# Four graph layers: the scores of attention layers 2 and 3 made inside the layer before, and both layers in one block

## Chip, cores, metric

One NeuronCore of one Trainium2 chip runs the whole program. The metric is device time in microseconds of one execution; smaller is better.

## The reference

Four layers over N = 8192 nodes with F = 128 features, each followed by `x = layernorm(x + layer(x))`. Layer 0 takes the maximum over neighbours. Layer 1 is graph attention with a threshold on the weights. Layers 2 and 3 are graph attention:

```python
Wh = h @ W
e = leaky_relu((Wh @ a_1)[:, None] + (Wh @ a_2)[None, :], 0.2)
attention = softmax(where(adj > 0, e, NEG), axis=1)
h_prime = attention @ Wh
return elu(h_prime)
```

Each row's score is a dot product of that row with `W @ a`, for `a_1` and for `a_2`; the column scores enter through factors that need their greatest value over all nodes.

## The kernel before

The node features live in `X`, 128 partitions by T = 64 tiles of 128 features. Rows of a 0/1 mask, transposed and in one byte, were written to DRAM (`mask_t`) by layer 0.

Engines here are PE (TensorE), DVE (VectorE), ACT (ScalarE), POOL (GpSimd) and SP, which issues most transfers. Each engine's order is written out by hand, and semaphores join them. Every layer is a `Phase`, which ends with barriers of all engines.

**Layer 1** (`threshold_layer`) has a preparing stage and then S = 8 strips of 1024 target rows. A strip walks 64 steps j. At each, DVE makes `w` (line 1481: the weights of tile j for 1024 targets) into a ring of six, and PE multiplies (line 1223). Beside it run the denominators of the next strip (ACT makes `above`, DVE masks it, PE adds it up) and the thresholds (ACT makes `u`, DVE masks it, line 1356). Between two strips POOL makes the next strip's limit in five small instructions (lines 1119 to 1129). PE turns the limits, ACT copies them to `ell`, makes `u`, and DVE masks `u` before the last two `w` of the old strip. The results of strip c are added to `X` during strip c + 1, where their mean and variance go to `stats` (DVE steps j = 38 to 42). Normalising them waits for the next layer.

**Layers 2 and 3** (`attention_layer`, called twice) each begin with a preparing stage, then have 16 chunks of 512 targets. The preparing stage loads W and a, and turns all of `X` on PE into `XT` (ACT copies it, 16 pieces). PE makes the scores of each tile from it (line 1572), with dummy matmuls between. In layer 2 it also normalises the 64 tiles (line 1630). DVE sums `XT` for the mean row (line 1654). It then takes the greatest score (line 1660), POOL joins the partitions, and ACT makes the factors `E` and `G`. In a chunk, DVE makes `w` (line 1888) into a ring of WR = 8, and PE multiplies by `GX` (line 1773). At j = 24, 28 and 38 DVE finishes the chunk before: `post`, `post_rest`, `standardise` (line 1868). In chunk 0 DVE also makes `GX` (`weigh`, line 1873). POOL makes `lone_part`, one instruction per chunk (line 1738). ACT is used little there.

Of the kernel before, what the change touches and what calls it, by code (L numbers as in the profile page):

```python
# [5 lines left out]
F32 = mybir.dt.float32  # L6
# [860 lines left out]
def threshold_layer(nc, W1, a_src, a_dst, mask_t, xt_rows, X, stats, rstd, ident, sel):  # L867

    with ExitStack() as ctx:
# [22 lines left out]
        post_bank = ctx.enter_context(nc.psum_tensor("post_bank", [P, H, CI], F32))  # L892
        den_in = [sem(f"den_in{b}") for b in range(2)]
# [8 lines left out]
        with ExitStack() as pctx:  # L902
            psb = lambda n, s: pctx.enter_context(nc.sbuf_tensor(f"{n}_1", s, F32))
            XT, WT, A3, U3, sdh = psb("XT", [P, N]), psb("WT", [P, F]), psb("A3", [P, 3]), psb("U3", [P, 3]), psb("sdh", [P, T, 3])
            B, rest, dm, nb, v = psb("B", [P, T]), psb("rest", [P, T]), psb("dm", [P, 1]), psb("nb", [P, 3]), psb("v", [P, T])
            banks = [ps[:, h, :] for ps in (acc, den_ps, row_ps, post_bank) for h in range(H)]
            w_in, step, eps_made, rstd_made = sem("w_in"), sem("prep_step"), sem("eps_made"), sem("rstd_made")
# [7 lines left out]
            def _(sp):  # L915
                sp.dma_start(Wn[:, :], W1).then_inc(w_in, 16)
                sp.dma_start(A3[:, 0:1], a_src).then_inc(w_in, 16)
                sp.dma_start(A3[:, 1:2], a_dst).then_inc(w_in, 16)
                for n in range(2):
                    load(sp, den_m, den_in, n)  # L920
# [13 lines left out]
            def _(pe):  # L934

                def weights():
# [4 lines left out]
                    pe.wait_ge(u_sb, 1)  # L941

# [31 lines left out]
                last.then_inc(sd_ps, 1)  # L974

            @block.scalar
            def _(act):
                nc.scalar.preload_act_table_set(LN_EXP)
                act.wait_ge(eps_made, 1)
                nc.scalar.activation(rstd[:, :], stats[:, :, 1], ACT.Ln, bias=epsc[:, 0:1]).then_inc(rstd_made, 1)  # L980
                act.wait_ge(rstd_made, 1)
                nc.scalar.activation(rstd[:, :], rstd[:, :], ACT.Exp, scale=-0.5).then_inc(rstd_made, 1)
                for g in range(NG):
                    act.wait_ge(tr, g + 1)
                    nc.scalar.activation(XT[:, g * CI:(g + 1) * CI], banks[g % 4][:, :], ACT.Copy).then_inc(ev, 1)
                act.wait_ge(nb_sb, 1)
# [3 lines left out]
                nc.scalar.activation(qcol[:, :], zcol[:, :], ACT.Exp, scale=-0.8).then_inc(egb, 1)  # L990

            @block.vector
            def _(dve):
# [10 lines left out]
                dve.wait_ge(rstd_made, 2)  # L1004
# [5 lines left out]
                for g in range(1, T // NORM):  # L1010
                    normalise(g)
                s.did(nc.vector.memset(tiny[:, :], TINY))
# [37 lines left out]
        xt = sb("xt", [P, W], F32)  # L1050
        above = sb("above", [P, AS, H, GT, CI], FP8)
# [60 lines left out]
        def _(pool):  # L1112
            for c in range(S):
# [901 lines left out]
```

## Time and profile before

| | us |
|---|---|
| median of 3 runs (4797.67 to 4809.75) | 4803.89 |
| the profiled execution | 4804.22 |
| its span | 4802.5 |
| PE busy (91% of the span) | 4376.7 |
| DVE busy (89%) | 4257.5 |
| ACT busy (47%) | 2267.8 |
| POOL busy (24%, nearly all in layer 0) | 1163.7 |

The span runs from the first to the last instruction. By the timeline, layer 0 ends at about 1617 us, layer 1's first products start at 1730 us, and its last at 2875 us. Layer 2's products run from 2941 to 3836 us and layer 3's from 3894 to 4789 us. An engine's busy share is a mean over stages that differ, so the stages are read one by one.

### The profile page before, as it was taken

The numbers are of one execution on the slowest core, as the hardware profiler recorded it, in microseconds if no ns is written. First come the engines' busy times: TensorE is split into PE (matmuls) and PEld (weight loads), VectorE is DVE, ScalarE is ACT, GpSimd is POOL, SyncE is SP. The second block draws the span as 40 slices with busy tenths as digits, with TensorE's granted clock in tenths as the row PEclk, the third lists the DMA queues.
The fourth block names the chain that finished last, engine by engine and source line by source line (L and its number), as shares of the span: only waits on it lengthen the run. The fifth ranks groups of instructions, "written<-read, shape, count | busy, mean of one in ns | idle before, by whom it ended". The sixth has DMA issues, their size and how long they took to land. (4 is left out here: it accounts for less than half of the span.)

```text
span 4802.5 us, 67836 instructions
## 1 busy us (share of the span) xinstructions
PE 4376.7 (91%) x22391; PEld 2133.7 (44%) x22391; DVE 4257.5 (89%) x7884; ACT 2267.8 (47%) x2494; POOL 1163.7 (24%) x1195
## 2 busy tenths in 40 slices
PE   5888888888888579999999998999999989999998
PEld 3444554444444324333443344444444454444444
DVE  7999999999999778888888888999999869999998
ACT  4677777677766398899888841000000010000000
POOL 6677677667677100000000000000000000000000
PEclk7999999999999789999999998999999989999999
DMA  8788888778876232333333212222222022222220
GB/s 318 264 275 270 267 275 273 257 260 276 266 265 211 98 132 106 118 119 127 111 117 115 109 57 113 82 76 75 82 83 81 3 111 79 79 83 104 83 84 7
DMA packets 181702, 709.78 MB, mean 148 GB/s; under 512 B 31168, under 2 KB 39872, under 8 KB 132224
## 3 DMA queue, kind: packets, MB, share of 16 engines
q1 hardware_dynamic: 110816, 566.01, 34.3%
q0 software_dynamic: 33760, 73.21, 4.7%
q10 hardware_dynamic: 36864, 67.13, 3.7%
q8 instruction: 158, 2.59, 0.2%
q14 instruction: 104, 0.85, 0.1%
HBM read 630.59 MB, written 79.82 MB: 148 GB/s over the span
## 5 line engine op out<-in xcount | busy, mean ns | idle before, releaser
L1773 PE MATMUL bank<-w,GX 128*128 128x512 f32 x4096 | 1768.1, 593 | 4.8 <-DVE w L1888 4.8
L1888 DVE SCALAR_TENSOR_TENSOR w<-q,E,m 128x512 f32<-128x512 f32 x2048 | 1471.8, 759 | 130.1 <-PE bank L1773 40.2
L1773 PEld LDWEIGHTS bank<-w,GX 128*128 128x128 f32 x4096 | 777.5, 190 | 975.2 <-issue 975.1
L367 POOL DMA_INDIRECT ring<-x_ext,idx x1051 | 1053.3, 1002 | 481.6 <-issue 329.7
L1223 PE MATMUL acc<-w,GX 128*128 128x512 f32 x2048 | 938.1, 604 | 67.5 <-DVE w L1481 64.3
L521 PE MATMUL sums<-lone,xs 128*128 128x512 fp8e4 x3000 | 744.9, 385 | 142.2 <-DVE top L625 127.9
L431 ACT ACTIVATE stage<-tp 128x1024 fp8e4<-128x1024 uint16 x512 | 523.1, 1023 | 424.6 <-PE tp L484 408.7
L625 DVE TENSOR_TENSOR top<-top,sums 128x512 f32<-128x512 f32 x968 | 618.4, 678 | 38.9 <-PE sums L521 38.3
L1481 DVE SCALAR_TENSOR_TENSOR w<-q,E,u 128x1024 f32<-128x1024 f32 x512 | 635.1, 1275 | 1.9 <-PE acc L1223 1.8
L1223 PEld LDWEIGHTS acc<-w,GX 128*128 128x128 f32 x2048 | 371.4, 190 | 566.0 <-issue 411.8
L416 ACT ACTIVATE lone<-first_ps 128x1024 fp8e4<-128x1024 f32 x512 | 521.2, 1018 | 38.3 <-PE first_ps L507 37.5
L521 PEld LDWEIGHTS sums<-lone,xs 128*128 128x128 bf16 x3000 | 276.9, 98 | 566.6 <-issue 278.6
L1254 ACT ACTIVATE above<-q,nd 128x1024 fp8e4<-128x1024 f32 x488 | 516.4, 1140 | 0.0
L1265 ACT ACTIVATE u<-ell,ndd 128x1024 fp8e4<-128x1024 f32 x448 | 478.0, 1140 | 43.6 <-DVE w L1481 43.2
L1785 ACT ACTIVATE num<-bank 128x512 f32<-128x512 f32 x32 | 19.1, 597 | 1005.4 <-PE bank L1773 1005.4
L1738 POOL TENSOR_TENSOR lone_part<-mean_w,nohas 128x512 f32<-128x512 f32 x32 | 37.5, 1174 | 1583.7 <-DVEq L1846 1560.8
L484 PE MATMUL tp<-ident_b,adjb 128*128 128x128 bf16 x4096 | 328.2, 226 | 76.1 <-DVE X L649 43.0
L507 PE MATMUL first_ps<-stage,firsts 128*128 128x512 fp8e4 x1022 | 312.0, 388 | 2.2 <-ACT lone L416 2.2
L484 PEld LDWEIGHTS tp<-ident_b,adjb 128*128 128x128 bf16 x4096 | 255.4, 101 | 109.3 <-DVE X L649 46.3
L630 DVE TENSOR_TENSOR ring<-ring 128x384 f32<-128x384 f32 (+2 forms) x512 | 260.8, 509 | 22.2 <-DMA ring<-x_ext,idx 17.7
L1789 ACT ACTIVATE ex<-ex 128x512 f32<-128x512 f32 x32 | 20.2, 630 | 540.6 <-DVE ex L1847 540.6
L1119 POOL TENSOR_TENSOR den<-den,qcol 128x8 f32<-128x8 f32 x8 | 9.5, 1193 | 1045.9 <-ACT den L1300 1045.9
(252 smaller groups left out, 3199.9 us busy)
## 6 DMA issues: line engine op xcount, KB each, us to landing
adjb<-in_adj SPq DMA_DIRECT2D x256, 1024.0 KB
m<-mask_t SPq DMA_DIRECT2D x128, 1024.0 KB, 4.9
mask_t<-stage ACTq DMA_DIRECT2D x256, 256.0 KB
den_m<-mask_t SPq DMA_DIRECT2D x64, 1024.0 KB, 7.0
keep_m<-mask_t SPq DMA_DIRECT2D x64, 1024.0 KB, 4.9
ring<-x_ext,idx POOLq DMA_INDIRECT x1051
z<-row_scores SPq DMA_DIRECT2D x30, 256.0 KB, 4.7
xt_rows<-XT SPq DMA_DIRECT2D x8, 512.0 KB, 4.0
```

What stands on the lines that cost most here:

```text
L367: pool.indirect_dma_start(ring[:, s, :], None, x_ext, bass.IndirectOffsetOnAxis(ap=idx[:, k, s:s + 1], axis=0)).then_inc(done, 16)
L416: nc.scalar.activation(lone[:, b, :, :], first_ps[:, :, :], ACT.Relu, saturate=False).then_inc(lone_made, 1)
L431: nc.scalar.activation(stage[:, q, e * TRB:(e + 1) * TRB, k * P:(k + 1) * P], tp[e % 2][:, :, :].bitcast(U16), ACT.Sign, saturate=False).t ...
L484: last = nc.tensor.transpose(tp[e % 2][:, i, :], low_half[:, j // PW, j % PW:j % PW + P], ident_b[:, :])
L521: last = nc.tensor.matmul(out[:, a, :], xs[:, part_, 2 * n + a, :], lone[:, b, a, :], start=(part_ == 0), stop=(part_ == 2))
L625: nc.vector.tensor_tensor(out=top[:, a, :], in0=top[:, a, :], in1=sums[:, a, :], op=ALU.max).then_inc(sums_used[a], 1)
L1223: last = nc.tensor.matmul(acc[:, h, :], GX[:, j, :], w[:, n % WR1, h, :], start=(j == 0), stop=(j == T - 1))
L1254: nc.scalar.activation(above[:, n % AS, :, i, :], qb[:, c % 2, :, :], ACT.Sign, bias=nd[:, j:j + 1], scale=-1.0, saturate=False).then_inc( ...
L1265: nc.scalar.activation(u[:, n % US, :, i, :], ell[:, c % 2, :, :], ACT.Sign, bias=ndd[:, j:j + 1], saturate=False).then_inc(keeps_made, 1)
L1481: nc.vector.scalar_tensor_tensor(out=w[:, n % WR1, :, :], in0=qb[:, c % 2, :, :], scalar=E[:, j:j + 1], in1=u[:, n // GT % US, :, j % GT, ...
L1773: last = nc.tensor.matmul(acc[b][:, :], GX[:, j, :], w[:, j % WR, :], start=(j == 0), stop=(j == T - 1))
L1888: nc.vector.scalar_tensor_tensor(out=w[:, j % WR, :], in0=q, scalar=E[:, j:j + 1], in1=m[:, b, j, :], op0=ALU.max, op1=ALU.mult).then_inc( ...
```

## The change

The preparing stages of layers 2 and 3 are gone, and both layers stand in one `Phase` and one block (`attention_layers`; l = 0 and 1). What they made is made elsewhere:

- **In layer 1's preparing stage**: W and a of layer 2 are loaded, and `U_next`, the product of W and a spread over all partitions, is made.
- **In layer 1's strips**: ACT makes `rstd` of strip c - 1 at j = 50 (`spread`). POOL runs `prepare_next` for a strip whose rows are final: it normalises eight tiles, adds them to a running sum and makes both scores by a product and halvings, 26 instructions. It follows the five limit instructions of strip c, for strip c - 2. One more call stands behind the loop. The eighth strip is left to the next phase, where DVE normalises it and makes the scores that the greatest value needs.
- **In layer 2's chunks**: POOL makes the two products of layer 3's scores and the running sum, three instructions a chunk, and ACT adds up the products in eight activations a chunk.
- **In chunk 0 of both layers**: PE turns the scores, makes the mean row, and in layer 2 also layer 3's weights. The masks of layer 3's first two chunks are loaded during layer 2's last two.

```diff
+def threshold_layer(nc, W1, a_src, a_dst, mask_t, xt_rows, X, stats, rstd, ident, sel, lastrow, following):
...
+            def prepare_next(c):
+
+                col = slice(c * KC, (c + 1) * KC)
+                pool.wait_ge(rstd_made, 2 * (c + 1))
+                pool.wait_ge(stats_made, KC * (c + 1))
+                for t in range(c * KC, (c + 1) * KC):
+                    nc.gpsimd.tensor_scalar(X[:, t, :], X[:, t, :], stats[:, t, 0:1], rstd[:, t:t + 1], ALU.subtract, ALU.mult).then_inc(rows_normed, 1)
+                pool.wait_ge(rows_normed, KC * (c + 1))
+                for i in range(2):
+                    half = slice(c * KC + i * TC, c * KC + (i + 1) * TC)
+                    pool.wait_ge(x_summed, 2 * c + i + 1)
+                    nc.gpsimd.tensor_tensor(out=x_sum[:, :, :], in0=x_sum[:, :, :], in1=X[:, half, :], op=ALU.add).then_inc(x_summed, 1)
+                for k in range(2):
+                    own.do(nc.gpsimd.tensor_tensor(out=prod[:, :, :], in0=X[:, col, :], in1=U_next[:, k, :].unsqueeze(1).to_broadcast([P, KC, F]), op=ALU.mult))
+                    h = F // 2
+                    while h > 1:
+                        own.do(nc.gpsimd.tensor_tensor(out=prod[:, :, 0:h], in0=prod[:, :, 0:h], in1=prod[:, :, h:2 * h], op=ALU.add))
+                        h //= 2
+                    own.do(nc.gpsimd.tensor_tensor(out=scores_next[:, k, col], in0=prod[:, :, 0], in1=prod[:, :, 1], op=ALU.add))
...
                 nc.gpsimd.tensor_tensor(out=limit[:, :], in0=over[:, :], in1=logs[:, :], op=ALU.add).then_inc(limit_made, 1)
+                if c >= 2:
+                    prepare_next(c - 2)
+            prepare_next(S - 2)
...
+                    if c > 0 and j == 50:
+                        spread(c - 1)
...
         @block.gpsimd
         def _(pool):
...
+            greatest(0)
+            pool.wait_ge(rows_normed, KC)
+            for k in range(2):
+                score(k, NC - 2 + k, 0, 0)
+            for k in range(2):
+                add_rows(0, NC - 2 + k, k + 1)
...
+            for c in range(NC - 1):
+                if c + 2 < NC:
+                    pool.wait_ge(post_used, c + 2)
+                    for_lone(0, c + 2, c % 2)
+                pool.wait_ge(x_normed, (c + 1) * TC)
+                pool.wait_ge(scored, OPENED + c * 2 * TC)
+                for k in range(2):
+                    score(k, c, 1, k)
+                add_rows(1, c, c + 3)
+            greatest(1)
...
         @block.tensor
         def _(pe):
...
+                    if first and j == 16:
+                        turn_scores(l)
+                        mean_of_rows(l)
+                    if first and j == 24:
+                        mean_of_products(l)
+                    if first and l == 0 and j == 36:
+                        turn_next_weights()
+                    if first and l == 0 and j == 44:
+                        score_rows()
...
         @block.vector
         def _(dve):
...
+            def greatest_score(l):
...
+                s.do(nc.vector.tensor_tensor(out=last_prod[:, 0:tiles, :], in0=X[:, at, :], in1=Us[l][:, 1, :].unsqueeze(1).to_broadcast([P, tiles, F]), op=ALU.mult))
+                s.do(nc.vector.tensor_reduce(scores[l][:, 1, at], last_prod[:, 0:tiles, :], axis=AXX, op=ALU.add))
+                if l:
+                    dve.wait_ge(scored, SCORED)
+                nc.vector.tensor_reduce(dms[l][:, :], scores[l][:, 1, :], axis=AXX, op=ALU.max).then_inc(next_dm, 1)
```

On POOL, in layer 1, these rows follow the limit of strip c in the changed kernel (`prod` and `scores` are the products and the scores of the next layer):

```order
L1179 TENSOR_TENSOR limit<-over,logs 128x8
L1148 TENSOR_SCALAR X<-X,stats,rstd 128x128 x8
L1153 TENSOR_TENSOR x_sum<-x_sum,X 128x512 x2
L1155 TENSOR_TENSOR prod<-X,U 128x1024
L1158 TENSOR_TENSOR prod<-prod 128x8x64
L1158 TENSOR_TENSOR prod<-prod 128x8x32
L1158 TENSOR_TENSOR prod<-prod 128x8x16
```

Before, the limit was the last row, and the first of the next strip's five came next.

On DVE, between layers 1 and 2, the kernel before has these rows between the statistics of the last strip and the first `w`:

```order
L1630 TENSOR_SCALAR X<-X,stats,rstd 128x128 x56
L1654 TENSOR_REDUCE zc<-XT 128x1
L1655 TENSOR_SCALAR zrep<-zc 128x128
L1658 COPY sdh<-bank_2 128x192
L1660 TENSOR_REDUCE dm<-sdh 128x1
L1663 TENSOR_SCALAR nb<-D 128x1 x2
```

The changed kernel has these in that place, and the same but for the first between layers 2 and 3:

```order
L2031 TENSOR_SCALAR X<-X,stats,rstd 128x128 x8
L1985 TENSOR_TENSOR last_prod<-X,U 128x1024
L1986 TENSOR_REDUCE scores<-last_prod 128x8
L1989 TENSOR_REDUCE dm_2<-scores 128x1
L1992 TENSOR_SCALAR nb_2<-D_2 128x1 x2
L1973 TENSOR_TENSOR GX<-X,G_2 128x8x127
```

The normalising of 56 tiles and the long sum left DVE, and the product and sum of the last tiles came.

## Rows read from the trace of the kernel before

**Rows 1.** Page, costliest groups: busy us, mean ns, idle before with its releaser.
```profile
L1773 PE MATMUL bank<-w,GX 128*128 128x512 f32 x4096 | 1768.1, 593 | 4.8 <-DVE w L1888 4.8
```

**Rows 2.** Windows: length, busy us of each engine (instructions), PEclk, DMA share, GB/s.
```profile
2160.00:2308.00 148.00, 139.32 (x578) 58.49 (x577) 125.94 (x134) 133.68 (x131) 4.90 (x5) 1.00 0.32 117
...
2999.00:3054.00 55.00, 55.00 (x136) 24.84 (x135) 50.62 (x86) 2.77 (x6) 1.14 (x1) 1.00 0.24 81
...
3836.00:3894.00 58.00, 40.23 (x307) 35.24 (x306) 19.12 (x41) 16.54 (x29) 0.38 (x1) 0.77 0.38 152
...
2940.00:2943.00 3.00, 2.07 (x3) 1.07 (x4) 2.97 (x5) 1.24 (x2) 0.00 (x0) 0.50 0.38 86
```

**Rows 3.** Timeline, layer 1 to layer 2: start us, length us, engine, line, operation [idle before].
```profile
2889.18 0.64 DVE L1442 BATCH_NORM_AGGREGATE stats<-bn 128x2 f32<-128x6 f32 x8
...
2893.39 2.14 DVE L1630 TENSOR_SCALAR X<-X,stats,rstd 128x128 f32<-128x128 f32 x8 [1.37 <-ACT rstd L1613]
...
2932.11 0.24 DVE L1660 TENSOR_REDUCE dm<-sdh 128x1 f32<-128x64 f32 x1
...
2933.21 0.38 ACT L1618 ACTIVATE E<-sdh,nb 128x64 f32<-128x64 f32 x1 [10.72 <-DVEq L1665]
...
2938.65 0.69 ACT L1802 ACTIVATE z<-bank,D 128x512 f32<-128x512 f32 x1 [1.03 <-PE bank L1753]
...
2940.03 1.42 DVE L1888 SCALAR_TENSOR_TENSOR w<-q,E,m 128x512 f32<-128x512 f32 x2 [1.99 <-ACT q L1807]
...
2940.93 2.04 PE L1773 MATMUL bank<-w,GX 128*128 128x512 f32 x2 [2.38 <-DVE w L1888]
```

**Rows 4.** Timeline, layer 2 to layer 3.
```profile
3844.37 1.12 DVE L1868 TENSOR_SCALAR X<-X,mv,rs 128x128 f32<-128x128 f32 x4 [0.60 <-ACT rs L1795]
...
3894.22 1.19 PE L1773 MATMUL bank<-w,GX 128*128 128x512 f32 x1 [2.38 <-DVE w L1888]
```

**Rows 5.** Groups by line, VectorE.
```profile
L1434 DVE SCALAR_TENSOR_TENSOR X<-hp,X 128x1024 f32<-128x1024 f32 x8 | 9.7, 1215 | 0.0
...
L656 DVE TENSOR_REDUCE codes<-X 128x4 f32<-128x512 f32 x16 | 10.8, 677 | 0.0
```

**Rows 6.** Timeline, POOL: before layer 1, in its first strip and in a later strip.
```profile
1562.57 19.73 POOL L404 TENSOR_TENSOR X<-X,adjb 128x512 f32<-128x512 f32 x15 [1.83 <-DMA ring<-x_ext,idx]
...
1718.61 0.21 POOL L1121 TENSOR_TENSOR den<-den,den 128x8 f32<-128x8 f32 x1
...
2299.41 1.12 POOL L1121 TENSOR_TENSOR den<-den,den 128x8 f32<-128x8 f32 x1
```

**Rows 7.** Timeline, four w instructions with a POOL instruction beside them, and without.
```profile
3072.69 1.15 POOL L1738 TENSOR_TENSOR lone_part<-mean_w,nohas 128x512 f32<-128x512 f32 x1 [54.67 <-DVEq L1846]
...
3072.86 3.52 DVE L1888 SCALAR_TENSOR_TENSOR w<-q,E,m 128x512 f32<-128x512 f32 x4
...
3798.60 2.73 DVE L1888 SCALAR_TENSOR_TENSOR w<-q,E,m 128x512 f32<-128x512 f32 x4
```

**Rows 8.** Timeline, the end of a strip of layer 1.
```profile
2303.04 1.06 POOL L1129 TENSOR_TENSOR limit<-over,logs 128x8 f32<-128x8 f32 x1
...
2311.47 1.23 DVE L1356 SCALAR_TENSOR_TENSOR u<-u,keep_m 128x1024 int32<-128x1024 int32 x1 [7.43 <-ACT u L1265]
...
2313.95 3.70 PE L1223 MATMUL acc<-w,GX 128*128 128x512 f32 x8 [1.00 <-DVE w L1481]
...
2328.16 1.23 DVE L1356 SCALAR_TENSOR_TENSOR above<-above,den_m 128x1024 int32<-128x1024 int32 x1 [5.29 <-DMA den_m<-mask_t]
```

**Rows 9.** Timeline, ScalarE late in the last strip of layer 1.
```profile
2842.78 4.27 ACT L1265 ACTIVATE u<-ell,ndd 128x1024 fp8e4<-128x1024 f32 x4 [2.69 <-DVE w L1481]
```

**Rows 10.** Timeline, one chunk of layer 2.
```profile
3005.46 1.05 PE L1761 MATMUL bank<-Wa,num 128*128 128x129 f32 x8
...
3030.74 17.77 DVE L1888 SCALAR_TENSOR_TENSOR w<-q,E,m 128x512 f32<-128x512 f32 x25
...
3048.75 13.49 DVE L1888 SCALAR_TENSOR_TENSOR w<-q,E,m 128x512 f32<-128x512 f32 x16 [0.24 <-PE bank L1773]
```

More of the change, by code:

```diff
@@ L1721, in _ @@
                     hold(sp, q_ready, it * 2 + b + 1)
[L1722 to L1732 removed]
+                    load_rows(0, it * 2 + b + 2, b)
@@ new lines, in _ @@
+                    masks(it * 2 + b, it * 2 + b + 2, b)
+            for b in range(2):
+                masks(NC - 2 + b, b, b)
+            turned(1)
+            sp.wait_ge(q_ready, NC)
+            load_rows(1, 1, 1)
+            with sp.Fori(0, NC // 2 - 1) as it:
+                for b in range(2):
+                    hold(sp, q_ready, it * 2 + (NC + b + 1))
+                    load_rows(1, it * 2 + b + 2, b)
+                    masks(it * 2 + (NC + b), it * 2 + b + 2, b)
+                    store(it * 2 + b)
@@ L1776, in _ @@
             w_in_order = Tally(pe, w_made)
-            chunks(pe, chunk, post)
+            for l in range(2):
+                if l:
+                    pe.wait_ge(num_ready, NC - 1)
+                    pe.wait_ge(eps_made, 3)
+                chunk(l, 0, 0, True)
+                with pe.Fori(0, NC // 2 - 1) as it:
+                    chunk(l, it * 2 + 1, 1, False)
+                    chunk(l, it * 2 + 2, 0, False)
+                chunk(l, NC - 1, 1, False)
+                post(l, NC - 1)
@@ L1807, in chunk, with sum_scores @@
                 nc.scalar.activation(qb[:, b, :], z[:, b, :], ACT.Exp, scale=-0.8).then_inc(q_ready, 1)
-                if not first:
-                    take(c - 1, 1 - b)
-                    expo(c - 1)
-                    spread(c - 1)
-            def end(c, b):
-                take(c, b)
-                expo(c)
-                spread(c)
-            nc.scalar.preload_act_table_set(LN_EXP)
-            written_out(chunk, end)
+            def sum_scores(l, parts, before):
+                for n, (k, c, kind) in enumerate(parts):
+                    act.wait_ge(prod_made, before + n + 1)
+                    for i in range(TC):
+                        t = c * TC + i
+                        nc.scalar.activation(prod[:, k, i, :], prod[:, k, i, :], ACT.Copy, accum_out=scores[l][:, kind, t:t + 1]).then_inc(scored, 1)
@@ L1907, in program @@
+            for t in range(T - KC, T):
+                nc.vector.tensor_scalar(X[:, t, :], X[:, t, :], stats[:, t, 0:1], rstd[:, t:t + 1], ALU.subtract, ALU.mult).then_inc(rows_normed, 1)
+            for l in range(2):
+                greatest_score(l)
+                for c in range(NC):
+                    chunk(l, c, c % 2)
+                post(l, NC - 1)
+                post_rest(l, NC - 1)
+                standardise(l, NC - 1)
 def program(nc, x, adj, W1, a1, W2, a2, W3, a3, out):
```

540 lines of the change are left out of this document (286 added, 254 removed).

## Prediction

> **What bounds the kernel now.** I read the page first, then the busy time by windows to find the stages, then the timeline at their borders.
>
> In layers 2 and 3 the page gives 1768.1 us to the products of 2048 steps, 0.863 us a step, and PE waited 4.8 us for them in all [rows 1]. A window inside a chunk shows PE busy for 55.00 of 55 us and DVE for 50.62 [rows 2]. So PE sets these chunks, and DVE has 4.4 us to spare in each.
>
> Between the layers PE does nothing of this. The last instruction of layer 1's tail on DVE ends at 2889.8 us and the first product of layer 2 starts at 2940.93 [rows 3]. Layer 2's tail ends at 3845.5 and layer 3 starts at 3894.22 [rows 4]. These two stretches, 51 and 49 us, are what the change attacks.
>
> In layer 1 a strip takes about 148 us, in which PE is busy for 139.32, ACT for 133.68 and DVE for 125.94 [rows 2]. No engine has much room. At the end of a strip DVE waits 7.43 us for `u`, masks it, makes the last two `w`, and PE, its ring run dry, waits 1.00 us for them [rows 8]. This place matters, because `prepare_next` starts there.
>
> **Layer 1 to layer 2.** The phase starts as before, and DVE's first eight tiles are normalised by 2893.39 + 2.14 = 2895.5 [rows 3]. Then come, one behind the other: the product of eight tiles, 1.22 (the form 128x1024 with two inputs), its sum, 2 x 0.68 = 1.36 [rows 5]; from the start of the greatest value to ACT's first factor 1.10; two factors, 0.7 together; from `z` to the first `w` 1.38; to the first product 0.90 [rows 3]. That is 6.7 us, so 2902.2. POOL has two products of rows queued behind `greatest(0)`, just when DVE wants its first `weigh`. I add 1.5 for that, about one POOL instruction. Layer 2 starts at 2903.7, and 2940.93 - 2903.7 = 37.2 us go.
>
> **Layer 2 to layer 3.** No phase ends here. From 3845.5: product of four tiles 0.6, sum 0.68, then the same 1.10 + 0.7 + 1.38 + 0.90, and 1.5 for POOL, together 6.9, so 3852.4. 3894.22 - 3852.4 = 41.8 us go. Both savings: 79.0 us. The row scores and the mean row aren't on this path: they are made inside chunk 0, and needed by chunk 1 some 50 us later. ACT and SP wait in line for them there, but the rows of chunk 1 need only a turn at j = 16 and two transfers.
>
> **What chunk 0 gains in work.** PE gets 18 short passes in layer 2 (one turn of scores, eight for the mean row, two for its product, seven for the next weights) and 11 in layer 3. Eight such passes take 1.05 us [rows 10], so 2.3 + 1.4 = 3.7 us. DVE loses POOL's extra instructions in the same chunk, but PE's extra work and its slow start cover them: its clock is granted at 0.50 just after the idle stretch before [rows 2], and I take that to be so in both kernels.
>
> **What POOL costs DVE.** This is the disputed term. A POOL instruction of 512 columns takes 19.73 / 15 = 1.32 us and one of eight columns 0.21 us with DVE elsewhere, but the same eight columns take 1.12 us beside DVE's masks and `w` [rows 6]. The two engines hold each other up. Four `w` take 2.73 us alone and 3.52 us with one POOL instruction of 512 columns beside them, so DVE loses 0.79 us [rows 7]. The eight-column instructions cost it nothing that I can see.
>
> The Trainium skill ("SBUF — State Buffer", section "SBUF: two separate sides") calls the port pair that DVE and POOL share an exclusive lock, held for the whole instruction. By it DVE would lose up to POOL's whole time with the port, more than my 0.79; the last rival is what that would do here.
>
> `prepare_next` on POOL, from rows 6 by a straight line (0.2 us and 0.0022 us a column): eight of 128 columns 0.45 each, two of 512 at 1.3, and for each of two scores 2.4 + 1.3 + 0.7 + 0.45 + five short ones 1.3. That is 3.6 + 2.6 + 12.3, with their waits some 20 us. It runs six times behind a limit. The limit ends at 2304.1 [rows 8]; the first ten instructions fit the stretch in which DVE is idle, but the 1024-column product runs from about 2311 to 2313, over the mask at 2311.47 (1.5 us late), and the 512-column halving meets the `w` behind it (0.8), the next halvings the second one (0.5). PE is waiting for exactly these, and ACT waits for PE. So I take 3 us a strip, 18 us in all. Later in the strip DVE waits 5.29 us for a mask [rows 8] and for ACT elsewhere, so I let the rest be absorbed. The bounds: nothing (DVE's idle takes it all), and 0.79 us per 512 columns for all of it with none absorbed; the 26 instructions hold some 6100 columns (8 x 128, 2 x 512 and 2 x 2032), so 9.4 us a strip and 57 us for six.
>
> The seventh call stands at the end of layer 1. It can start when ACT has made `u` of the last group but one, at 2847.1 [rows 9]. Slowed to one short instruction per DVE instruction it would end near 2877, ahead of 2889.8 [rows 3], so it costs nothing. If it didn't, each us beyond would be a us of the kernel. `spread` puts two short activations in a place where ACT waits for `w`, and costs nothing. Layer 1's preparing stage gets three small loads and a turn: 0.5 us.
>
> **Layer 2's chunks.** Three POOL instructions follow `standardise`, 3 x 0.79 = 2.4 us. After that place DVE makes 25 `w` in 17.77 us, 0.711 each, where PE takes 0.863, and then waits for PE [rows 1, 10]. So it had been 25 x 0.15 = 3.8 us behind a full ring of 8 x 0.863 = 6.9, with 3.1 us left. 2.4 fits in 3.1, and in DVE's 4.4 us a chunk. I take 0.5 us in all for the first chunks. ACT's eight activations a chunk find ACT idle (busy for 2.77 us of 55).
>
> **The sum.** 4804.2 - 79.0 + 3.7 + 18 + 0.5 + 0.5 = 4747.9. The profiled execution is within 0.4 us of the median, so nothing is corrected: 4748 us, 1.2% faster.
>
> **The rivals.**
>
> 1. POOL in layer 1 is free. DVE is idle for 148 - 125.94 = 22 us of a strip, and a ring of six `w` stands between it and PE. Against it, PE already waits at the very place. 4748 - 18 = 4730.
> 2. POOL costs its full price in layer 1, 9.4 us a strip and none absorbed: 4748 - 18 + 57 = 4787. For it: all three engines are over 85% busy. Against it: DVE is idle for some 6 of the first 7 us in which `prepare_next` runs, and waits again later.
> 3. The ring of eight runs dry in layer 2. If a product of real rows costs DVE the whole 1.3 us, three cost 3.9 against 3.1: 0.8 us in 14 chunks, 4748 + 11 = 4759. It lies in the forecast's own range.
> 4. Slower: the port is held for all of POOL's 20 us, and the strip grows by it, since the late masks delay the loads that SP issues behind them and so the next masks. Six strips give 120: 4748 - 18 + 120 = 4850. It decides from (79.0 - 4.7) / 6 = 12.4 us a strip upward. Against it: 0.79 of 1.15 us is what one such instruction cost, and part of the work meets an idle DVE.
>
> **How the numbers follow.** The forecast, with its own range of 4735 to 4772 (about 1 to 7 us a strip, the third rival in it), gets 0.68. POOL free gets 0.12, the full price 0.11, and the fourth rival or any other way to end near the old time or above 0.09. A range from 4722 to 4788 leaves out the last, half of the full price, and a little below: a faster restart of PE would put the free case under 4730. A change of 0.3%, 14 us, is about what a measurement of this kernel can tell from none. Faster (below 4790) holds the forecast, the free case and most of the full price: 0.87. Within 0.3% I give 0.06, slower 0.07.
>
> **What would show it.** The start of layer 2's products should lie 13 to 14 us behind the last tail instruction of layer 1, and layer 3's 7 us behind layer 2's. The strips of layer 1 should show 148 us grown to about 151 from the second on, with a longer PE wait for `w` just behind each limit. PE should be busy throughout the chunks of layer 2, and their length stay 55.6 us. I am wrong if a strip grows by over 6 us, if POOL's last `prepare_next` ends after DVE's last statistics, or if layer 2's chunks are longer than layer 3's.

## The result and the profile after

The changed kernel takes 4757.6 us (median of 4 runs, 4745.5 to 4762.7) where the kernel before takes 4804.4: the ratio is 0.990, with a 95% interval of 0.9877 to 0.9922. That is 47 us less. Run again beside other experiments it took 4756.2 (0.9904, 0.9888 to 0.9921). The forecast was 4748, its range 4722 to 4788. Two executions among the experiments, one of e1's kernel (7800 us) and one of e4's (8445 us), fell in a slow state and are left out of every median.

The profiled execution of the changed kernel is its fastest run, 4745.5 us with a span of 4742.9. Of its costliest groups these lines of the page answer to [rows 1]; columns are busy us, mean ns, and idle time before with its releaser.

```profile
L1802 PE MATMUL bank<-w,GX 128*128 128x512 f32 x4096 | 1769.7, 593 | 27.4 <-DVE w L2015 27.4
L2015 DVE SCALAR_TENSOR_TENSOR w<-q,E,m 128x512 f32<-128x512 f32 x2048 | 1478.5, 773 | 101.1 <-PE bank L1802 35.7
...
L1276 PE MATMUL acc<-w,GX 128*128 128x512 f32 x2048 | 947.6, 609 | 77.3 <-DVE w L1544 74.4
...
L1687 POOL TENSOR_TENSOR prod<-X,U_next 128x512 f32<-128x512 f32 x31 | 227.3, 7352 | 230.6 <-DVE X L1968 223.6
```

The products of layers 2 and 3 (L1802) cost what they did. The two stretches between layers shrank. The timeline from layer 1 to layer 2, for [rows 3]:

```profile
2902.90 0.64 DVE L1505 BATCH_NORM_AGGREGATE stats<-bn 128x2 f32<-128x6 f32 x8
...
2905.01 0.53 POOL L1700 MEMSET x_sum<- 128x512 f32 x1 [5.02 <-POOLq L113]
...
2911.57 0.22 DVE L1989 TENSOR_REDUCE dm<-scores 128x1 f32<-128x64 f32 x1
...
2916.56 0.38 POOL L1698 PARTITION_ALL_REDUCE D<-dm  x1 [11.03 <-issue]
...
2920.11 13.47 PE L1802 MATMUL bank<-w,GX 128*128 128x512 f32 x26 [13.84 <-DVE w L2015]
...
2928.43 3.36 POOL L1687 TENSOR_TENSOR prod<-X,U 128x512 f32<-128x512 f32 x2 [11.49 <-issue]
```

The tail ends at 2903.54 and the first product starts 16.6 us later, where it was 51.1. One thing stands out: the maximum `dm` is ready at 2911.79, but POOL's all-reduce starts at 2916.56, and POOL stood for 11.03 us before it with "issue" as the reason. From layer 2 to layer 3, for [rows 4]:

```profile
3826.63 1.11 DVE L1968 TENSOR_SCALAR X<-X,mv,rs 128x128 f32<-128x128 f32 x4 [0.60 <-ACT rs L1834]
...
3829.58 0.38 POOL L1698 PARTITION_ALL_REDUCE D<-dm  x1 [21.95 <-DVE dm L1989]
...
3833.12 2.90 PE L1802 MATMUL bank<-w,GX 128*128 128x512 f32 x3 [12.42 <-DVE w L2015]
```

5.4 us from tail to product, where it was 48.7. What was paid for this shows in layer 1. The groups of lines from the second strip's limit to the tail's end, before (L1223) and after (L1276), with the same columns as the page:

```profile
L1223 PE MATMUL acc<-w,GX 128*128 128x512 f32 x1832 | 836.3, 602 | 55.2 <-DVE w L1481 52.2 <-ACT num L1236 2.6
```

```profile
L1276 PE MATMUL acc<-w,GX 128*128 128x512 f32 x1832 | 845.2, 608 | 65.5 <-DVE w L1544 62.8 <-ACT num L1289 2.6
```

This stretch grew from 1034.2 to 1054.4 us, by 20.2. PE waits 10.3 us more for `w`, and its same 1832 products take 8.9 us longer. The second number is not a wait: the products themselves ran slower. The border of a strip, in the timeline, for [rows 8]:

```profile
2303.10 6.24 POOL L1148 TENSOR_SCALAR X<-X,stats,rstd 128x128 f32<-128x128 f32 x8
2309.42 3.48 POOL L1153 TENSOR_TENSOR x_sum<-x_sum,X 128x512 f32<-128x512 f32 x2
2312.86 3.33 POOL L1155 TENSOR_TENSOR prod<-X,U 128x1024 f32<-128x1024 f32 x1
...
2310.49 1.29 DVE L1419 SCALAR_TENSOR_TENSOR u<-u,keep_m 128x1024 int32<-128x1024 int32 x1 [7.44 <-ACT u L1318]
2311.70 7.77 DVE L1544 SCALAR_TENSOR_TENSOR w<-q,E,u 128x1024 f32<-128x1024 f32 x3
...
2314.04 1.98 PE L1276 MATMUL acc<-w,GX 128*128 128x512 f32 x4 [2.08 <-DVE w L1544]
2317.32 1.98 PE L1276 MATMUL acc<-w,GX 128*128 128x512 f32 x4 [1.30 <-DVE w L1544]
...
2333.77 3.63 PE L1276 MATMUL acc<-w,GX 128*128 128x512 f32 x4 [2.05 <-DVE w L1544]
```

Three `w` take 7.77 us beside POOL's additions and products, against some 3.7 without. Four products of PE take 1.98 us at 2317, but 3.63 at 2333.77. The windows around that place (length, busy us of PE, PEld, DVE, ACT and POOL, PEclk, DMA share, GB/s) say why:

```profile
2324.00:2333.70 9.70, 7.33 (x29) 4.14 (x28) 5.59 (x6) 9.70 (x11) 9.23 (x7) 1.00 0.85 324
2333.70:2337.10 3.40, 3.33 (x4) 1.17 (x4) 3.40 (x4) 3.40 (x5) 3.17 (x4) 0.50 0.00 0
2337.10:2345.00 7.90, 7.90 (x46) 3.10 (x46) 7.90 (x11) 7.90 (x8) 0.33 (x1) 1.00 0.14 31
```

Right behind the third wait the granted clock stands at 0.50, which is 1.2 in place of 2.4 GHz, for 3.4 us, and PE loses half of them, 1.7 us. In slices of 2 us the changed kernel shows six such stretches in layer 1, the kernel before none until layer 1's tail. Six times 1.7 is 10.2 us, and PE's busy time in the stretch from the second limit to the tail's end rose by 9.9 us, from 968.9 to 978.8, of which 8.9 are on the products.

So the change of the profiled execution, part by part: layer 1 +20.2; its end -34.5; layer 2's chunks +3.1; layer 2's end -43.3; layer 3 +2.0. Together -52.5 us. The execution of before that was profiled came 6.5 us later into layer 1's second strip, with nothing of the change in that part; over all the profiles of this study that moment lies between 1846.5 and 1862.9 us. It is left out of every comparison of parts below; the medians contain it.

### The profile page after: what moved, and what is told of

Same layout as the page of the kernel before. It is cut to its first block and busy times, and to the rows that moved or that the text cites. A ratio compares the mean times of both kernels' runs of the same rounds, so it can differ in the third digit from the quotient of the medians.

```text
span 4742.9 us, 66895 instructions
## 1 busy us (share of the span) xinstructions
PE 4303.7 (91%) x21712; PEld 2072.7 (44%) x21839; DVE 4294.5 (91%) x7813; ACT 2293.9 (48%) x2747; POOL 1668.6 (35%) x1430
## 5 line engine op out<-in xcount | busy, mean ns | idle before, releaser
L1802 PE MATMUL bank<-w,GX 128*128 128x512 f32 x4096 | 1769.7, 593 | 27.4 <-DVE w L2015 27.4
L1802 PEld LDWEIGHTS bank<-w,GX 128*128 128x128 f32 x4096 | 776.7, 190 | 993.8 <-issue 989.6
L1276 PE MATMUL acc<-w,GX 128*128 128x512 f32 x2048 | 947.6, 609 | 77.3 <-DVE w L1544 74.4
L1544 DVE SCALAR_TENSOR_TENSOR w<-q,E,u 128x1024 f32<-128x1024 f32 x512 | 665.2, 1336 | 0.1
L1276 PEld LDWEIGHTS acc<-w,GX 128*128 128x128 f32 x2048 | 373.6, 191 | 580.6 <-issue 409.2
L1169 POOL TENSOR_TENSOR den<-den,qcol 128x8 f32<-128x8 f32 x8 | 5.6, 704 | 883.5 <-ACT den L1361 883.5
L1687 POOL TENSOR_TENSOR prod<-X,U_next 128x512 f32<-128x512 f32 x31 | 227.3, 7352 | 230.6 <-DVE X L1968 223.6
L1828 ACT ACTIVATE ex<-ex 128x512 f32<-128x512 f32 x32 | 20.2, 631 | 563.8 <-DVE ex L1944 563.8
```

The costliest lines, as they stand in the source:

```text
L1276: last = nc.tensor.matmul(acc[:, h, :], GX[:, j, :], w[:, n % WR1, h, :], start=(j == 0), stop=(j == T - 1))
L1544: nc.vector.scalar_tensor_tensor(out=w[:, n % WR1, :, :], in0=qb[:, c % 2, :, :], scalar=E[:, j:j + 1], in1=u[:, n // GT % US, :, j % GT, ...
L1802: last = nc.tensor.matmul(acc[b][:, :], GX[:, j, :], w[:, j % WR, :], start=(j == 0), stop=(j == T - 1))
```

## The experiments

All start from the changed kernel. "Strips" are the distances between the first POOL instructions of one limit and the next (L1169), the second to the seventh. "Layer 1" runs from the second limit to the end of the tail on DVE; "products" and "waits" are the busy and the idle time of PE's `acc` group in it, as in the two lines above; "layer 2" runs from its first product to layer 3's. "Dips" are the stretches at half clock inside layer 1's strips, most of them 3.4 us long; one each in e11 and e5 and two in e3 are twice that.

```
kernel              strips (us)                          layer 1  products  waits  dips  layer 2  median
before              147.7 147.6 147.6 148.5 147.5 147.5   1034.2    836.3    55.2     0    953.3  4804.4
changed             147.6 150.5 150.4 151.8 150.9 150.6   1054.4    845.2    65.5     6    913.0  4757.6
e11 changed again   147.6 150.5 150.2 151.8 152.7 150.3   1055.7    844.5    67.1     5    920.6  4756.2
e2 no POOL work     147.7 147.7 147.7 149.0 147.7 147.8   1035.3    837.1    55.0     1    920.6  4743.5
e7 standardise only 147.6 147.6 147.9 149.1 147.6 148.4   1036.1    836.3    56.5     0    920.8  4734.8
e12 no products     147.7 148.8 150.8 151.8 148.8 150.4   1048.8    844.4    61.7     5    913.0  4752.5 (one run)
e3 products twice   147.7 154.7 155.2 155.8 155.1 154.4   1083.5    853.0    84.5    10    913.1  4789.5
e4 23 us later      147.7 153.9 153.8 155.1 153.8 153.8   1070.4    845.7    81.5     4    913.2  4766.4
e5 turned maximum   147.7 150.4 150.4 151.7 152.6 150.4   1056.3    843.9    68.2     4    920.7  4749.2
e6 products first   147.7 147.9 148.9 149.2 147.9 147.8   1046.7    838.4    64.2     1    920.7  4742.7
e8 e5 and e6        147.7 147.8 147.8 149.2 147.8 148.1   1045.7    838.9    64.0     1    920.6  4743.4
e9 all three        147.7 147.7 147.7 149.2 147.9 147.9   1045.3    838.9    63.8     1    913.9  4735.6
e10 e9, all-reduce  147.6 147.7 147.9 149.2 147.9 147.9   1045.3    839.1    63.4     1    913.4  4744.5
```

Ratios to the kernel before, with their intervals: e1 (e12's kernel, timed) 0.989, 0.9872 to 0.9907; e2 0.9861, 0.9836 to 0.9886; e3 0.9965, 0.9951 to 0.9978; e4 0.9922, 0.99 to 0.9943; e5 0.9878, 0.9861 to 0.9894; e6 0.9866, 0.9849 to 0.9882; e7 0.9843, 0.9826 to 0.986; e8 0.9866, 0.9846 to 0.9885; e9 0.9854, 0.9837 to 0.987; e10 0.9879, 0.9862 to 0.9895; the changed kernel as above.

### Is the loss in layer 1 POOL's, and of which work?

**e2, none of it.**

```diff
-                    nc.gpsimd.tensor_scalar(X[:, t, :], ... ).then_inc(rows_normed, 1)
+                pool.sem_inc(rows_normed, KC)
-                    nc.gpsimd.tensor_tensor(out=x_sum[:, :, :], ... ).then_inc(x_summed, 1)
+                    pool.sem_inc(x_summed, 1)
-                for k in range(2):
-                    own.do( ... products, halvings ... )
```

> The changed kernel with all seven calls of prepare_next emptied (no standardising, no running sum, no products; their semaphores are still raised, in their places), so layer 2 works on rows that are not standardised and on scores of zero. This leaves ACT's spread in layer 1 and the new borders as they are. Theory A and Rival C of the first kernel: strips of layer 1 back at 147.5 to 147.8, the last strip with the tail back at 147.8, in all 20 us less than the changed kernel, about 4737 us. Rival D, part of the 20 us in layer 1 isn't POOL's but comes of ACT's two added operations at step 50 or of DVE's separate semaphore steps: strips stay at 148.3 or more. POOL's all-reduce at the border of layers 1 and 2 should no longer start late, if what delayed it was the work before it: then another 4.8 us less; if it is a change of POOL's configuration of fixed length behind the border, it stays.

The strips are back at 147.7 to 149.0 and layer 1 is back at 1035.3: all but 1.1 of the 20.2 us are POOL's work. The all-reduce still started late, 10.89 us behind POOL's memset, so the delay isn't the work ahead of it. The median fell by 14 us and not by 20. In the two traces layer 2 took 7.6 us more; more on this below. How many of the timed executions had that isn't known.

**e1 and e12, without products and halvings.**

```diff
                     nc.gpsimd.tensor_tensor(out=x_sum[:, :, :], ... ).then_inc(x_summed, 1)
-                for k in range(2):
-                    own.do( ... products, halvings ... )
```

> The changed kernel with the products and their halvings left out of prepare_next (both score columns of all seven calls, so layer 2's scores are zeros from a memset; the standardising and the running sum stay). Each call of POOL falls from about 34 to about 10 us. In the changed kernel a strip of layer 1 takes 150.4 to 150.9 us where it took 147.5 to 147.7 before, and the last strip with the tail 4.9 us more. Theory A, that of the prediction (what counts is what meets DVE's mask and the refilling of the ring in the first 15 us of a strip, and the product and the halvings are what meets them): the strips fall to about 148.2, the total by some 14 to 17 us against the changed kernel. Rival B, the eight standardising operations, which come first, carry the delay: the strips stay at 149.5 or more, the total falls by less than 8 us. Rival C, every microsecond of POOL costs alike wherever it lies (3.0 us for 34, 0.09 each): strips at 148.5, total -14. A and C are told apart by the two other kernels of this call.

Timed, it took 4751.5 us, only 6 below the changed kernel. Neither theory A nor C had given that, and B, which had, falls with e7 below. Its strips are read from e12, the same kernel:

> The kernel without products and halvings once more, for a trace at full clock: each call of prepare_next keeps its eight standardising operations and the two 512-column adds of the running sum (products and scores left out, scores zero). Theory F (only POOL's two-input operations hold DVE up): the two adds take 3.5 of the 27 to 28 us of two-input work, so strips at 147.9 to 148.2 against 147.6 to 147.9 without them and 150.4 to 150.9 with all. Rival: the first two-input operations behind the border carry most of the loss, as they meet the mask: strips at 149 or more.

Theory F had given 147.9 to 148.2, and that isn't what came: the strips are of two kinds, 148.8 twice and 150.4 to 151.8 three times. The rival is near. The five strips with a call average 150.12 us, 2.15 above e2's 147.97, where the changed kernel's 150.83 are 2.86 above. So two of POOL's 18 two-input operations, the first two behind the border, carry three quarters of the loss in a strip. DVE was busy for 886.3 us in layer 1, only 7.4 more than without POOL's work (878.9 in e2), while layer 1 is 13.5 us longer.

The two kinds differ in the clock. The 148.8 have no dip, the others have one or two. At the border the first three `w` take 4.67 us in e12, and 3.67 before:

```profile
2624.93 4.67 DVE L1538 SCALAR_TENSOR_TENSOR w<-q,E,u 128x1024 f32<-128x1024 f32 x3
```

```profile
2312.62 3.67 DVE L1481 SCALAR_TENSOR_TENSOR w<-q,E,u 128x1024 f32<-128x1024 f32 x3
```

POOL's additions make one of them 1.0 us late. That is enough to make PE's wait at the border 2.04 to 2.29 us, where it is 1.00 without them. So a strip grows by 1.1 us where no dip follows, and by 2.6 to 3.1 where one or two do. Here are three of these six borders:

```profile
2176.13 5.40 PE L1270 MATMUL acc<-w,GX 128*128 128x512 f32 x8 [2.29 <-DVE w L1538]
...
2478.47 3.70 PE L1270 MATMUL acc<-w,GX 128*128 128x512 f32 x8 [2.05 <-DVE w L1538]
...
2627.27 5.40 PE L1270 MATMUL acc<-w,GX 128*128 128x512 f32 x8 [2.05 <-DVE w L1538]
```

Eight products in 5.40 us at the first and the third, and in 3.70 at the second: the dip's 1.7 us can be read off the row. A dip came at four of the six borders, and the length of the wait doesn't decide it, since one wait of 2.05 had none behind it and the next of 2.05 had one. What decides isn't settled.

**e7, the standardising alone.**

```diff
-                    nc.gpsimd.tensor_tensor(out=x_sum[:, :, :], ... ).then_inc(x_summed, 1)
+                    pool.sem_inc(x_summed, 1)
-                for k in range(2):
-                    own.do( ... products, halvings ... )
```

> The changed kernel with only the eight standardising operations left in each call of prepare_next: running sum, products and halvings are left out (scores and running sum zero from a memset). Theory F: these operations cost DVE nothing, strips of layer 1 at 147.6 to 147.9, as with all of POOL's work left out, total about 4743 us, some 14 below the changed kernel. Rival H: 6.2 of 34 us of the work remain, so strips at 148.2 and 4 us more in all than with none of it.

Strips at 147.6 to 149.1 and layer 1 at 1036.1 us: POOL's one-input operations cost next to nothing, whatever POOL's busy time. Rival H falls.

**e3, products and halvings twice.**

```diff
-                for k in range(2):
+                for k in (0, 1, 0, 1):
                     own.do(nc.gpsimd.tensor_tensor(out=prod[:, :, :], ...
```

> The changed kernel with the products and halvings of each prepare_next made twice (the same result is written a second time). Each call grows from about 34 to about 57 us; the added 23 us lie 35 to 58 us behind the start of a strip. Theory A (the loss is at the strip's border alone): strips grow by less than 0.5 us over the changed kernel's 150.4 to 150.9, the total by less than 4 us beside what the last call adds, which now ends after layer 1's tail (2899.99 in the changed kernel, tail to 2903.54) and holds up the border to layer 2 by some 20 us or more, since beside unbroken two-input operations of DVE it runs three times slower. Rival C (every microsecond of POOL costs alike): strips grow by 2.0 us, to 152.6. The prediction's fourth rival (DVE stands for as long as POOL has an operation in hand): strips grow by 23 us.

The added 23 us of POOL cost 3.8 to 4.9 us a strip, more than the first 34 did. Theory A falls in its strict form: the border isn't the only place where the loss is. The prediction's fourth rival falls too: DVE doesn't stand for all of POOL's time. The last call ended behind the tail and the first product came 27 us after it, as said.

**e4, the same work 23 us later.**

```diff
                 if c >= 2:
+                    pool.wait_ge(w_made, c * T + 10)
                     prepare_next(c - 2)
```

> The changed kernel with one wait added ahead of the first six calls of prepare_next: POOL begins when DVE has made the tenth tile of the strip, some 23 us behind the strip's first, when the ring of tiles is full again. The work is the same 34 us. Theory A: the strips fall from 150.4 to 150.9 to about 148.2 and the total by about 12 us. Rival C: the strips and the total stay. Rival E, the work costs more in the middle of a strip, where DVE's two-input operations follow each other without a gap and POOL gets the port late: POOL's call takes over 60 us, and strips grow.

The opposite of theory A: the strips grow to 153.8 to 155.1, and the call costs 6.2 us instead of 3. Its timeline shows POOL's instructions and DVE's beside them:

```profile
2501.22 16.53 POOL L1148 TENSOR_SCALAR X<-X,stats,rstd 128x128 f32<-128x128 f32 x8 [35.65 <-DVE w L1545]
2517.84 4.08 POOL L1153 TENSOR_TENSOR x_sum<-x_sum,X 128x512 f32<-128x512 f32 x2
2521.88 3.34 POOL L1155 TENSOR_TENSOR prod<-X,U 128x1024 f32<-128x1024 f32 x1
```

```profile
2504.59 3.73 DVE L1545 SCALAR_TENSOR_TENSOR w<-q,E,u 128x1024 f32<-128x1024 f32 x3
...
2518.49 2.29 DVE L1545 SCALAR_TENSOR_TENSOR w<-q,E,u 128x1024 f32<-128x1024 f32 x1
2520.71 2.28 DVE L1420 SCALAR_TENSOR_TENSOR u<-u,keep_m 128x1024 int32<-128x1024 int32 x1
2522.92 5.59 DVE L1545 SCALAR_TENSOR_TENSOR w<-q,E,u 128x1024 f32<-128x1024 f32 x2
```

Beside POOL's standardising three `w` take 3.73 us, as ever. Beside its additions and products each takes 2.3 to 2.8: the two engines go in turn, DVE's 1.2 us behind POOL's 1.1, which is the lock for a whole instruction that the prediction cited. The Trainium skill ("SBUF — State Buffer", section "Who interferes with whom") says that a DVE instruction with two SBUF inputs contends with a POOL instruction that reads SBUF. For POOL's two-input instructions these rows agree. The one-input ones read SBUF as well, and here they waited for DVE (16.53 us for eight that take 6.24 at the border) but did not hold it up.

**e6, products first.** If the border is the cheap place, because DVE stands there for 7.4 us, then the two-input work should lie there, and the standardising behind it:

```diff
-                if c >= 2:
-                    prepare_next(c - 2)
-            prepare_next(S - 2)
+                if c >= 3:
+                    multiply(c - 3)
+                if c >= 2:
+                    standardise(c - 2)
+            multiply(S - 3)
+            standardise(S - 2)
+            multiply(S - 2)
```

> The changed kernel with POOL's order turned round in layer 1: behind a strip's limit it now adds, multiplies and halves the rows that it standardised one strip earlier (call c - 3), and standardises the rows of call c - 2 behind that; the last strip does both. The work is the same, its place is moved by 6.3 us: in the changed kernel POOL standardises in the 7.4 us in which DVE stands at a strip's border and begins the two-input operations when DVE is back. The earlier kernels showed strips at 147.6 to 147.9 without POOL's work, 150.4 to 150.9 with it, 155 with the products twice, and 153.9 with the work begun 23 us late, where each of DVE's two-input operations beside one of POOL's took 2.3 us instead of 1.2 while beside POOL's standardising it stayed at 1.2. Theory F (a two-input operation of POOL holds up a two-input operation of DVE for its whole length, one-input operations don't): six us more of POOL's two-input time fall where DVE waits, so the strips fall to about 149.3, the total by 7 to 12 us. Rival H (only the busy time of POOL counts, whatever the operation): strips stay at 150.4 to 150.9.

```profile
2301.14 2.61 POOL L1155 TENSOR_TENSOR x_sum<-x_sum,X 128x512 f32<-128x512 f32 x2
2303.71 2.36 POOL L1157 TENSOR_TENSOR prod<-X,U 128x1024 f32<-128x1024 f32 x1
2306.15 6.22 POOL L1160 TENSOR_TENSOR prod<-prod 128x512 f32<-128x512 f32 x6
...
2308.56 1.29 DVE L1425 SCALAR_TENSOR_TENSOR u<-u,keep_m 128x1024 int32<-128x1024 int32 x1 [7.43 <-ACT u L1324]
```

The strips fall to 147.8 to 149.2, further than the 149.3 expected, and close to e2's. DVE is hardly less delayed (it is busy for 910.0 us in layer 1, against 914.6), but PE's waits in the first 40 us of a strip add up to 4.3 or 4.4 us in place of 6.1 in the first three (2.08, 1.30, 0.24, 0.40 and 2.05), where they were 3.0 before, and there is one dip in place of six. Products fall from 845.2 to 838.4 us. Of the 12.5 us of loss that are left, 9.4 lie in the last strip, in which the products of two calls now run in mid-strip: 157.2 us from its limit to the tail's end, against 147.8 before.

### The start of layer 2

**e5, the maximum without POOL.**

```diff
-            greatest(0)
             pool.wait_ge(rows_normed, KC)
+            pool.wait_ge(w_made, 8)
...
+                    pe.wait_ge(next_dm, 1)
+                    nc.tensor.transpose(banks[6][:, 0:P], dms[0][:, 0:1].to_broadcast([P, P]), ident[:, :]).then_inc(dm_turned, 1)
...
+                    dve.wait_ge(dm_turned, 1)
+                    nc.vector.tensor_reduce(Ds[0][:, 0:1], banks[6][:, 0:P], axis=AXX, op=ALU.max).then_inc(next_d, 1)
```

> The changed kernel with layer 2's greatest score made without POOL: PE turns the 128 partial maxima (one 128x128 transpose) and DVE reduces the row, in place of partition_all_reduce; POOL's score products and sums of that border wait for eight made tiles instead, so that they start about where they did. In the changed kernel the all-reduce began at 2916.56, 4.8 us after its input was ready at 2911.79, 11.0 us after POOL's memset of 2905.01, and the first product came 16.6 us after layer 1's last tail instruction. Theory G: those 11 us are POOL's change of configuration for the all-reduce and nothing else, so without it the first product comes 13 us after the tail or sooner, 3 to 4 us less, and POOL's next products need no 11.5 us of change back either. Rival: the 5 us are the way of the semaphores between DVE, POOL and ACT at the start of a block, and stay whoever makes the maximum: first product still 16 to 17 us after the tail. Either way the total moves by less than 5 us, which five rounds hardly tell; the two traces do.

```profile
2924.93 0.22 DVE L1993 TENSOR_REDUCE dm<-scores 128x1 f32<-128x64 f32 x1
2925.71 0.29 DVE L1996 TENSOR_REDUCE D<-bank 128x1 f32<-128x128 f32 x1 [0.56 <-PE bank L1790]
...
2929.17 7.05 PE L1806 MATMUL bank<-w,GX 128*128 128x512 f32 x12 [3.49 <-DVE w L2022]
```

The tail ended at 2916.90, so the first product comes 12.3 us behind it, 4.3 earlier. Of theory G this shows that the delay comes with the all-reduce. That it is a change of POOL's configuration isn't shown. The total, 4749.2, is 8 us below the changed kernel with intervals that overlap.

**e11, the changed kernel again.**

> The changed kernel itself, unaltered, once more as the measure for the two others of this call and for two things that single executions showed. Theory: strips of layer 1 at 150.4 to 150.9 as before, first product of layer 2 at 16.6 us after the tail; of chunk 0 in layer 2 either PE waits 1.2 us in all, where POOL's four operations alternate with DVE's, as in the first look at it, or 7.5 us, where POOL's come to wait behind unbroken runs of DVE's, as in most of the experiments; the one or the other is decided by which of the two engines asks first, by less than 0.1 us. Rival: in the unaltered kernel it's always the 1.2 us, since the experiments' edits alone moved the phase. Median 4754 to 4762 us.

The waits of 7.7 us came, in the unaltered kernel: its rival falls. POOL and DVE in chunk 0 here and, in the second fence, in the first trace of the same kernel:

```profile
2926.20 9.47 POOL L1687 TENSOR_TENSOR prod<-X,U 128x512 f32<-128x512 f32 x2 [10.55 <-issue]
...
2926.88 1.24 DVE L1974 COPY GX<-G 128x8 f32<-128x8 f32 x1
2928.04 5.38 DVE L2015 SCALAR_TENSOR_TENSOR w<-q,E,m 128x512 f32<-128x512 f32 x8
...
2937.04 0.30 PE L1760 MATMUL bank<-ident,scores 128*64 128x128 f32 x1 [2.73 <-ACT prod L1855]
2942.27 2.04 PE L1767 MATMUL bank<-inv_n,x_sum 128*128 128x128 f32 x8 [4.93 <-POOL x_sum L1693]
```

```profile
2928.16 0.17 DVE L1974 COPY GX<-G 128x8 f32<-128x8 f32 x1
2928.24 9.44 DVE L2015 SCALAR_TENSOR_TENSOR w<-q,E,m 128x512 f32<-128x512 f32 x8
```

The eight `w` take 5.38 us in one and 9.44 in the other. In the first trace POOL's product came during a `w` and the engines took turns: POOL was done early, DVE late, PE waited 1.2 us. Here POOL's came in at DVE's small copy (1.24 us in place of 0.17), and its next ones waited for the end of each run of `w`: 6.5 us for two additions, and PE's passes at step 16 waited for them. That the order of asking decides is my reading of these two; why one request is served in turn and another at the end of the run isn't settled. It went the slow way in six of the ten traces with PE's readings in their place, and costs 7.6 us of layer 2 (920.6 against 913.0).

Not all of the 7.6 us is waiting. Each of these six traces shows a stretch of 6.83 us at half clock that begins in PE's waits, and none of the other four does. In e11 (length, busy us of PE, PEld, DVE, ACT and POOL, PEclk, DMA share, GB/s):

```profile
2938.92:2945.75 6.83, 3.48 (x10) 2.54 (x11) 0.75 (x2) 0.28 (x1) 3.13 (x2) 0.50 0.66 208
```

There the eight short passes take 2.04 us in place of 1.06, and the sixteen products behind them 7.85 in place of 7.03, together 1.8 us.

**e8, products first and the turned maximum.** The edits of e6 and e5.

> The two edits of this call together: POOL's products first, and the maximum turned by PE. If both of their theories hold, the total is the sum of the two, some 10 to 15 us below the changed kernel's 4757.6, so 4743 to 4748 us. If the products done beside a strip's border delay the mask of the next strip there, it stays within 4 us of the changed kernel.

4743.4 us (4733.4 to 4749.8), no better than e6 alone, though its trace has both effects (strips 147.8 to 149.2, first product 12.3 us behind the tail). It had the slow kind of chunk 0, as e6 had.

**e9 and e10, PE's readings later.**

```diff
-                    if first and j == 16:
+                    if first and j == (32 if l == 0 else 16):
...
-                    if first and j == 24:
+                    if first and j == (38 if l == 0 else 24):
-                    if first and l == 0 and j == 36:
+                    if first and l == 0 and j == 43:
...
-                    if first and l == 0 and j == 44:
+                    if first and l == 0 and j == 52:
```

> Three edits on the changed kernel: POOL's products first in layer 1 (strips 147.8 to 149.2 in an earlier kernel of these), layer 2's maximum turned by PE (first product 12.3 us after the tail in place of 16.6), and PE's readings of POOL's results in layer 2's first chunk moved from steps 16 and 24 to 32 and 38, so that POOL's late products and sums find PE not waiting (0 in place of the 7.5 us that the two other edits together showed). Theory: 4743.4 us of the kernel with the first two edits less 7, so 4734 to 4739 us, 20 us below the changed kernel. Rival: the wait isn't PE's own loss but is made up for later in the chunk by the ring of made tiles, and the time stays at 4743.

> As the kernel with all three edits, but the all-reduce stays with POOL. Theory: 4742.7 us of the kernel with POOL's products first alone, less 7 for PE's waits in layer 2's first chunk: 4736 us; so some 4 us above the one with all three, less than rounds can tell, but first product 17 us after the tail in the trace against 12. Rival: as for all three, the time stays at 4743.

e9 takes 4735.6 us (4727.0 to 4738.8). Beside it on the same chip the changed kernel took 4756.2: 20.6 us less, and the two ranges don't touch. Layer 2 took 913.9 us although POOL's four operations were of the slow kind (26 us), and it has no stretch at half clock behind its first 4 us, so in the other traces PE's wait was lost time and not made up for. That is the evidence of one trace. Against e8, which lacks only the later readings, the median is 8 us lower, but the intervals of the ratios overlap. e10 took 4744.5, with layer 2 at 913.4: by its time the rival came, no gain over e6's 4742.7. Its trace had POOL's operations of the quick kind, so it says nothing on the readings. It stands 9 us above e9 where 4 were expected. In the traces the two differ by 5.1 us between tail and first product (12.3 and 17.4), by 3.2 ahead of layer 1's second limit, where no edit reaches, and by 0.5 the other way in layer 2; the rest of the 9 isn't settled.

## Why the prediction was right, and where it wasn't

**The border of layers 1 and 2**, forecast 13.9 us and 37.2 saved: 16.6 and 34.5. The chain of steps was right but for one. "From the start of the greatest value to ACT's first factor 1.10" came from a row in which POOL had long been ready. Here POOL had just done a memset, and its all-reduce came 11.0 us behind that, of which 4.8 were on the path. The 1.5 us for POOL's products beside the first `weigh` weren't due: they came 11.5 us behind the all-reduce. e5 shows that most of the 4.8 go with the all-reduce (4.3 earlier).

**The border of layers 2 and 3**, forecast 6.9 us and 41.8 saved: 5.4 and 43.3. The 1.5 us for POOL again weren't due. Both borders: 77.8 us saved, forecast 79.0.

**POOL in layer 1**, forecast 18 us with bounds of 0 and 57: 20.2 and, the second time, 21.5. The size was right, and that was in part luck, since the steps behind it held only in part. The call takes 34 us beside DVE, not 20. "The product, 1.5 us late, and the halvings 0.8 and 0.5": the mask came on time, and the three `w` behind it took 4 us longer, but what PE lost by it was 10.3 us of waits over the layer, and as much again by half clock behind them, of which the prediction had nothing, though it had read the 0.50 behind the idle stretch of a border. The place was right, though not the instructions: the prediction let the two additions fit in DVE's idle stretch, and the second of them ran into the first `w` (e12). "I let the rest be absorbed" holds only where the call stands: e4 and e3 show that the same work in mid-strip costs double. That the port is given by the kind of instruction (e7 against e12), not by columns or busy time, wasn't in it either; 0.0022 us a column priced the standardising, which is free, like the products.

**The seventh call** was said to end at 2877 and cost nothing. It ended at 2899.99, since its eight standardising instructions took 19.89 us beside DVE, 3.5 us ahead of the tail's end. It ran beside the tail. The last strip took 4.9 us more than before, the others 2.8 to 3.4, so it cost some 2.

**Chunk 0's passes**, 3.7 us, and 0.5 for layer 2's chunks: 5.1 in the first trace. In the second 7.6 more, by POOL's late products and sums and the half clock behind PE's waits. The prediction saw that ACT and SP "wait in line" for the row scores and that they weren't needed for 50 us, and missed that PE's own turn of them at step 16 stops PE. This is a term left out, not one that was mis-sized, and e9's trace shows its price.

**Layer 2's chunks** kept their 55.8 us, so the third rival didn't happen. PE is never held up there, though POOL's products take 7.4 us each on average. The first rival (POOL free) isn't what came; with only the standardising left to POOL (e7) layer 1 is within 2 us of it, and e6's strips come near to it with all of the work. The second (57 us) and the fourth (120) fall with e3: even with the products twice it is 49.

The total, 47 us saved and 56 forecast: the terms above are -77.8 + 20.2 + 5.1 = -52.5 in one trace. In the other they are +21.5 for layer 1 and 7.6 more for layer 2, which gives -43.6. The median lies between the two.

## What to carry to other kernels

Before work is given to an idle POOL, sort it by inputs: one-input instructions can run beside DVE at any place, two-input ones belong where DVE waits anyway, and should start with that wait, so that the first of them don't run over its end. A wait of PE that looks small should be priced with what the clock does behind it: here a wait of 2 us often cost 1.7 more. And a result that another engine makes should be read as late as its use allows, since an in-order engine that reads it early turns a harmless delay into its own.

## What the runs showed of the hardware that I had not expected

- At the border of layers 1 and 2 POOL stood for 10.70 to 11.86 us between its memset and the all-reduce (11.03 in the first trace, 10.70 in e3, 11.86 in e10), and for 10.55 to 11.97 between the all-reduce and its next product. At the next border the way back took 7.06, and the way there was hidden in a wait of 21.95.
- PE's granted clock fell to 0.50 for 3.4 us behind waits of about 2 us in the midst of dense work, six times in one layer, and rose again while PE worked on. Behind other waits as long (2.08 at 2314.04) it stayed at 1.00. Behind 7.7 us of waits in chunk 0 it was 0.50 for 6.8 us.
- Eight one-input instructions of POOL, 128x128 each with two scalars a row, took 6.24 us with DVE idle and beside it 12.3, 16.5 or 19.9, and didn't slow it. Two-input ones of 512 columns made DVE's take 2.3 us in place of 1.2.
- The same kernel, started again, can fall into another pattern of POOL and DVE from a shift of less than 1 us, worth 7.6 us of 4750.
